# Cross attention in a decoder layer: passing two chunks through each stage together, and an output projection ordered by input chunk

## The chip, the cores and the metric

One core of one Trainium2 chip. The metric is the device time of one execution of the whole program, in microseconds (us). The engines are PE (matrix multiply; PEld is its weight load), DVE, ACT and POOL (elementwise and reductions) and SP (DMA issue). They run their own instruction streams and meet only at semaphores.

## The reference

A post-norm decoder layer on x (8 batches of 256 rows of 128): a state-space block, then cross attention, then six window-attention layers with feed-forward parts. Only the cross attention is touched. For each batch it computes, with 16 heads of 64:

```
lat = layernorm(latents, ln_l_w, ln_l_b)
ctx = layernorm(context, ln_c_w, ln_c_b)
q = (lat @ Wq).reshape(b, n, H, D).transpose(0, 2, 1, 3)
kv = ctx @ Wkv
...
attn = jnp.einsum('bhnd,bhsd->bhns', q, k) * scale
attn = jnp.clip(attn, -11.0, 11.0)
attn = jax.nn.softmax(attn, axis=-1)
out = jnp.einsum('bhns,bhsd->bhnd', attn, v)
out = out.transpose(0, 2, 1, 3).reshape(b, n, INNER)
return out @ Wo + bo
...
x = _layernorm(x + _L0_xattn_ref(x, ctx_1024, ...), axis=-1)
```

## The kernel before

The three blocks run one after the other; at the end of each, all engines meet. The cross-attention block is a software pipeline, written out by hand for each engine, over 64 chunks g: 8 batches b of 8 chunks c, a chunk being two heads (128 of the 1024 inner columns). All of it is in 32-bit floats. The names used below for the stages of a chunk on PE are these:

- P(g), `project`, L966 and L967: q and k of the chunk, two matmuls of 128x256 on the full 128x128 array, into one of two shared PSUM banks psM. ACT copies the bank to qk (`copy_qk`, L852).
- S(g), `scores`, L982: four matmuls of 256 columns, each on 64 rows of the array, so that two heads run side by side. ACT takes the exponential into E (`exponentials`, L845, two instructions), DVE clips it (`clip`, L899), and POOL adds the two key tiles into Es (L794).
- T(g), `times_v`: four matmuls with weights of 64 columns (L997), two side by side, then two with a matrix of ones (L1001) that sum the rows. DVE takes the reciprocal and multiplies (`normalise`, L903 and L904), which fills OT and counts O_free.
- V, `project_v`, L973: one 512-column matmul on the full array, once in each chunk with c of 4 to 7 for the next batch; ACT copies it (L836).
- OP, `out_projection`, L1012: 2x8 matmuls of 128 columns per batch, from OT and wo. DVE adds the result to res (`residual`, L909), takes moments (L47, L51), and `finish` (L918) writes the batch back. TR, `transpose_rows`, L958, prepares the next batch from `hats` (L893), which needs `statistics` (L47, L51) and ACT's `deviation` (L818, L819).

In iteration g PE does P(g+1), S(g), T(g-1). At the start of a batch, OP for the first tile of rows of the batch before comes at the end of the iteration with c = 1, and for the second tile at c = 2. E, Es, qk and psO have two buffers each, psS has four banks. The table `fills` lists everything that is put into the two psM banks, in PE's order; entry k goes into bank k mod 2, and PE may start it only when the entry before it in that bank has been read out (`bank`, `place`).

Of the kernel before, what the change touches and what calls it, by code (L numbers as in the profile page):

```python
# [680 lines left out]
def cross_attention_block(nc, xall, ident, eps_col, inputs, window):  # L681
# [9 lines left out]
    R = 2 * TPB  # L691
    LOADS = 16 * 7
    CHUNKS = B * NC
    LO, HI = float(np.exp(-11.0)), float(np.exp(11.0))

    with ExitStack() as ctx:
        def sb(name, shape, dt=F32):
            return ctx.enter_context(nc.sbuf_tensor(name, shape, dt))
# [48 lines left out]

        block = ctx.enter_context(nc.Block())

        fills = [(0, "cat"), (0, "qk0")]  # L750
        for g in range(CHUNKS + 1):
            b, c = divmod(g, NC)
            if g + 1 < CHUNKS:
                fills.append(((g + 1) // NC, f"qk{(g + 1) % NC}"))
            if g == 0:
                fills += [(0, f"v{n}") for n in range(4)]
            if c == 1 and b >= 1:
                fills.append((b - 1, "wo"))
            if c == 3 and b + 1 < B:
                fills.append((b + 1, "cat"))  # L760
            if c >= 4 and b + 1 < B:
                fills.append((b + 1, f"v{c - 4}"))
        fills.append((B - 1, "wo"))
        place = {f: (k % 2, k // 2) for k, f in enumerate(fills)}

        def wait_fill(eng, b, name):
# [16 lines left out]
        @block.gpsimd  # L783
        def _(pool):
            pool.memset(ones[:, :], 1.0).then_inc(Es_ready, 1)
            pool.memset(window.xsA[0:1, 0, 64:D], 0.0)
            pool.wait_ge(loaded, LOADS)

            def sum_of_tiles(g):
                pool.wait_ge(E_ready, 2 * g + 2)  # L790
                if g >= 2:

                    pool.wait_ge(O_full, g - 1)
                pool.tensor_tensor(Es[:, g % 2, :, :], E[:, g % 2, :, 0, :], E[:, g % 2, :, 1, :], ALU.add).then_inc(Es_ready, 1)  # L794
# [12 lines left out]
            pool.wait_ge(window.loaded, 32)  # L807
            pool.tensor_scalar(window.base_tab[:, :, 0, :, :], window.base_tab[:, :, 0, :, :], 8.0, None, ALU.mult)

        @block.scalar  # L810
        def _(act):
# [27 lines left out]
            def exponentials(g):  # L839
                for j in range(2):  # L840
                    act.wait_ge(S_full, 2 * g + j + 1)
                    if j == 0 and g >= 2:

                        act.wait_ge(O_full, g - 1)
                    act.activation(E[:, g % 2, j, :, :], psS[(2 * g + j) % 4][:, :, :], ACT.Exp, scale=DH ** -0.5).then_inc(E_exp, 1)  # L845
# [8 lines left out]
            deviation(0)  # L854
            scale_transposed(0)
            copy_qk(0)
            for g in range(CHUNKS + 1):
                b, c = divmod(g, NC)
                if g + 1 < CHUNKS:
                    copy_qk(g + 1)  # L860
                if g < CHUNKS:
                    exponentials(g)
                if g == 0:
                    for n in range(4):
                        evacuate_v(0, n)
                if c == 1 and b + 1 < B:
                    deviation(b + 1)
                if c == 3 and b >= 1:
                    deviation2(b - 1)
                if c == 3 and b + 1 < B:  # L870
                    scale_transposed(b + 1)
                if c >= 4 and b + 1 < B:
                    evacuate_v(b + 1, c - 4)
            deviation2(B - 1)

        @block.vector
        def _(dve):
# [18 lines left out]
            def clip(g):  # L896
                for j in range(2):
                    dve.wait_ge(E_exp, 2 * g + j + 1)
                    dve.tensor_scalar(E[:, g % 2, j, :, :], E[:, g % 2, j, :, :], LO, HI, ALU.max, ALU.min).then_inc(E_ready, 1)  # L899

            def normalise(g):
                dve.wait_ge(O_full, g + 1)
# [1 line left out]
                dve.tensor_tensor(OT[:, g // NC % 2, g % NC, :], psO[g % 2][:, 0, :], rden[:, g % 2, :], ALU.mult).then_inc(O_free, 1)  # L904

            def residual(b):
                ps, free = wait_fill(dve, b, "wo")
                dve.wait_ge(res_ready, b + 1)
                dve.tensor_tensor(res[:, :, :], res[:, :, :], ps[:, 0:TPB * D].rearrange("p (t d) -> p t d", d=D), ALU.add).then_inc(free, 1)  # L909

            def moments2(b):
                wait_evacuated(dve, b, "wo")
# [7 lines left out]

            statistics(0)
            hats(0)
            for g in range(CHUNKS + 1):
                b, c = divmod(g, NC)
                if c == 2 and b >= 1:
# [7 lines left out]
                if c == 2 and b + 1 < B:  # L933
                    hats(b + 1)
                if c == 2 and b >= 1:
                    moments2(b - 1)
                if c == 4 and b >= 1:
                    finish(b - 1)
            residual(B - 1)
            moments2(B - 1)  # L940
# [3 lines left out]
        def _(pe):  # L944
# [41 lines left out]
            def times_v(g):  # L986
                b, c = divmod(g, NC)
                pe.wait_ge(E_ready, 2 * g + 2)
                if c == 0:
                    for n in range(4):  # L990
                        wait_evacuated(pe, b, f"v{n}")
                if g >= 2:

                    pe.wait_ge(O_free, g - 1)
                for kt in range(TPB):
                    for j in range(2):
                        pe.matmul(psO[g % 2][j * DH:(j + 1) * DH, 0, :], V1[:, b % 2, kt, 2 * c + j, :], E[:, g % 2, j, kt, :],  # L997
                                  start=(kt == 0), stop=(kt == TPB - 1), skip_group_check=True)
# [19 lines left out]
            for g in range(CHUNKS + 1):  # L1018
# [10 lines left out]
                if g >= 1:  # L1029
# [3 lines left out]
                if c == 3 and b + 1 < B:  # L1033
# [979 lines left out]
```

## Time and profile before

| what | value |
|---|---|
| median of 3 timed runs | 2367.09 us (2366.22 to 2367.36) |
| the profiled execution, its own time | 2364.26 us |
| span of its trace | 2362.5 us |
| PE busy share of the span | 93% |
| cross attention, about | 321 to 623 us of the span |

The profile page gives, for the whole span, busy time and instruction count of each engine. Everything else is read from the stretch of the cross attention: the timeline (instructions in order of time, with start and length), the table of stretches, and the list of waits. In the timeline, runs of like matmuls are merged into one row; a row ends with a modelled tail, so distances are taken from start to start. A float matmul is shown as two records, so that `x8` of L982 is a whole S.

### The profile page before, as it was taken

Reading aid. Unit: us, or ns where it says so; the run is one execution under the profiler, and the core shown is the slowest. Engines: PE = TensorE matmul, PEld = TensorE weight load, DVE = VectorE, ACT = ScalarE, POOL = GpSimd, SP = SyncE. Lnnn points to the kernel's source line nnn. Section 1 sums busy time; section 2 is a strip of 40 time slices with the busy share of each in tenths; the row PEclk is TensorE's granted clock in tenths of the full one; section 3 lists DMA queues with packets and bytes.
Section 4 is the critical chain, followed back from the end, with each engine's and each line's share of the span. In section 5 each row is a group of like instructions: output and inputs, shape, how many; then the busy total and the mean of one; then the engine's idle time right before and its main releaser. Section 6 shows DMA issues by size and latency. Waiting matters only on the chain. (4 is left out here: it accounts for less than half of the span.)

```text
span 2362.5 us, 70312 instructions
## 1 busy us (share of the span) xinstructions
PE 2204.0 (93%) x26385; PEld 1467.1 (62%) x26385; DVE 1860.9 (79%) x2680; ACT 1707.2 (72%) x3299; POOL 1648.2 (70%) x1553
## 2 busy tenths in 40 slices
PE   5889779999799999999999999999999999999996
PEld 3555446666456666666666666666666666666664
DVE  4899957777678878888888888888888887888884
ACT  5889734544377787787787787787778778778774
POOL 4777833333478778778788787787787787787872
PEclk8999989999999999999999999999999999999997
DMA  2311210000022222222222222222222222322221
GB/s 74 113 58 66 72 52 2 1 1 1 20 63 67 55 78 67 59 74 67 65 69 67 69 64 67 73 60 67 77 55 68 79 54 68 79 53 72 75 53 52
DMA packets 103196, 140.36 MB, mean 59 GB/s; under 512 B 63072, under 2 KB 64096, under 8 KB 102752
## 3 DMA queue, kind: packets, MB, share of 16 engines
q1 hardware_dynamic: 103136, 139.57, 21.8%
q8 instruction: 36, 0.59, 0.1%
q14 instruction: 24, 0.20, 0.0%
HBM read 56.39 MB, written 1.31 MB: 24 GB/s over the span
## 5 line engine op out<-in xcount | busy, mean ns | idle before, releaser
L1802 PE MATMUL f_psA<-f_W,f_xT 128*128 (+1 forms) x1152 | 600.7, 631 | 21.1 <-DVE f_m L1607 13.4
L1607 DVE TENSOR_TENSOR f_m<-f_psA,f_tab 128x1024 f32<-128x1024 f32 x384 | 461.1, 1222 | 119.5 <-ACT f_sq L1468 106.3
L1357 POOL TENSOR_TENSOR f_Pr<-f_Pr,f_rden 128x384 f32<-128x384 f32 x384 | 311.0, 831 | 226.2 <-DVE f_rden L1586 226.2
L1385 POOL TENSOR_TENSOR f_qkr<-f_qkr,f_rn 128x1024 f32<-128x1024 f32 x192 | 361.2, 1902 | 0.2 <-POOL f_rn L1393 0.2
L1802 PEld LDWEIGHTS f_psA<-f_W,f_xT 128*128 128x128 f32 x1152 | 188.3, 189 | 162.9 <-issue 112.5
L1468 ACT ACTIVATE f_sq<-f_psA 128x512 f32<-128x512 f32 x384 | 228.0, 594 | 78.6 <-PE f_psA L1802 75.7
L1773 PEld LDWEIGHTS f_psO<-f_PT,f_V 96*64 96x64 f32 x6144 | 203.7, 138 | 96.5 <-issue 88.4
L1375 POOL TENSOR_TENSOR f_qkr<-f_m 128x512 f32<-128x512 f32 x192 | 244.1, 1271 | 8.2 <-DVE f_m L1607 8.2
L1376 POOL TENSOR_TENSOR f_qkr<-f_m 128x512 f32<-128x512 f32 x192 | 244.5, 1273 | 0.0
L1773 PE MATMUL f_psO<-f_PT,f_V 96*64 96x64 f32 x6144 | 232.1, 228 | 1.8 <-ACT f_PT L1443 1.8
L794 POOL TENSOR_TENSOR x_Es<-x_E 128x512 f32<-128x512 f32 x64 | 81.0, 1266 | 205.8 <-DVE x_E L899 205.8
L1622 DVE TENSOR_REDUCE f_ssq<-f_sq 128x32 f32<-128x2048 f32 x96 | 218.5, 2276 | 0.0
L1460 ACT ACTIVATE f_Pr<-f_Pr 128x768 f32<-128x768 f32 x192 | 162.2, 845 | 55.4 <-DVE f_Pr L1580 53.8
L1869 PE MATMUL f_psO<-f_W,f_oT 128*128 (+1 forms) x1536 | 196.9, 281 | 0.8 <-ACT f_oT L1456 0.8
L284 POOL TENSOR_TENSOR m_Hs<-m_Hs,m_Cb 128x1024 f32<-128x1024 f32 x64 | 151.3, 2370 | 64.4 <-DVE m_Hs L472 64.4
L1452 ACT ACTIVATE f_Vt<-f_psA 128x512 f32<-128x512 f32 x192 | 114.5, 597 | 112.0 <-PE f_psA L1802 107.1
L1580 DVE TENSOR_TENSOR f_Pr<-f_psS,f_mx 128x768 f32<-128x768 f32 x192 | 183.8, 957 | 10.7
L1573 DVE TENSOR_REDUCE f_mx<-f_psS 128x8 f32<-128x768 f32 x192 | 178.3, 929 | 14.3 <-PE f_psS L1741 8.6
L1869 PEld LDWEIGHTS f_psO<-f_W,f_oT 128*128 128x128 f32 x1536 | 178.7, 191 | 7.3 <-issue 0.9
L1584 DVE TENSOR_REDUCE f_den<-f_Pr 128x8 f32<-128x768 f32 x192 | 179.9, 937 | 3.9 <-ACT f_Pr L1460 3.9
L1417 POOL TENSOR_SCALAR f_hatC<-f_xsC,f_momC,f_rstdC 128x128 f32<-128x128 f32 x96 | 77.1, 803 | 136.9 <-ACT f_rstdC L1544 136.9
L1806 PE MATMUL f_psD<-f_xnT,f_W 128*128 128x256 f32 (+1 forms) x576 | 163.6, 395 | 1.4 <-issue 0.8
(167 smaller groups left out, 4894.6 us busy)
## 6 DMA issues: line engine op xcount, KB each, us to landing
f_V<-f_Vt SPq DMA_DIRECT2D x96, 384.0 KB, 4.2
f_V<-f_Vt SPq DMA_DIRECT2D x96, 256.0 KB, 3.6
f_W<-in_f_W SPq DMA_DIRECT2D x48, 344.0 KB, 3.4
m_Cb<-m_BC_rows SPq DMA_DIRECT2D x64, 256.0 KB, 3.1
f_W<-in_f_W SPq DMA_DIRECT2D x48, 296.5 KB, 4.0
f_V<-f_Vt SPq DMA_DIRECT2D x48, 128.0 KB, 5.3
f_xsA<-xall SPq DMA_DIRECT2D x97, 32.0 KB
f_xsA<-xall SPq DMA_DIRECT2D x97, 31.8 KB
```

Source lines behind the costliest of these rows:

```text
L1357: pool.tensor_tensor(pv, pv, rv.unsqueeze(3).broadcast_to([P, 2, 2, KEYS]), ALU.mult).then_inc(Pr_ready[g][j], 1)
L1375: pool.tensor_tensor(qv[:, :, 0, :], mv[:, 0, :, 0, :], mv[:, 1, :, 1, :], ALU.add)
L1376: pool.tensor_tensor(qv[:, :, 1, :], mv[:, 0, :, 1, :], mv[:, 1, :, 0, :], ALU.add).then_inc(rot_done[j], 1)
L1385: pool.tensor_tensor(qv, qv, rv.unsqueeze(3).broadcast_to([P, 2, GH, DH]), ALU.mult).then_inc(qkr_ready[g], 1)
L1468: act.activation(sq[:, n * 512:(n + 1) * 512], psA[n % 2][:, :], ACT.Square).then_inc(squared[n], 1)
L1580: dve.tensor_tensor(Pr[:, g, :, :].rearrange("p (a c) k -> p a c k", a=2), S4, mb, ALU.subtract).then_inc(S_free[g], 1)
L1584: dve.tensor_reduce(den[:, g, :], Pr[:, g, :, :], axis=AX.X, op=ALU.add).then_inc(den_done[g], 1)
L1607: dve.tensor_tensor(m12[:, j, :, half].rearrange("p m (h d) -> p m h d", d=DH), psA[n % 2][:, :].rearrange("p (h d) -> p h d", d=DH).unsqu ...
L1622: dve.tensor_reduce(ssq[:, :], sq[:, :].rearrange("p (h d) -> p h d", d=DH), axis=AX.X, op=ALU.add).then_inc(ssq_ready, 1)
L1773: ins = pe.matmul(psO[(h % 2) * DH:(h % 2) * DH + DH, h // 2, half * HQ:(half + 1) * HQ], V96[:, tile, half, hh_ * DH:(hh_ + 1) * DH], PT[ ...
L1802: pe.matmul(psA[n % 2][:, :], xT[:, t, :], weights(i, W_QKV + n * 512, 512), start=True, stop=True).then_inc(A_full[n_fill], 1)
L1869: ins = pe.matmul(psO[:, 0, :], oT[:, t, c, :], weights(i - 1, W_O + c * D, D), start=(c == 0), stop=(c == CH - 1))
```

## The change

Chunks pass the stages in pairs. In iteration g (now in steps of two) PE does S(g), S(g+1), T(g-2), T(g-1), P(g+2), P(g+3), then TR or two V where a batch has them. E has four buffers (ES = 4) where it had two. OP stands as one piece at the start of the iteration with c = 2; it goes over the eight input chunks in order, each time for both tiles of rows, and each tile has a psM bank of its own (`wo0`, `wo1`). It waits for both banks first and then for each chunk's O_free. The orders of `fills`, ACT and DVE follow; DVE does `clip(g)`, `normalise(g-2)`, `clip(g+1)`, `normalise(g-1)`, has `hats` before `residual` at c = 2, and `residual` is two instructions.

```diff
-        E = sb("x_E", [P, 2, 2, TPB, L])
+        E = sb("x_E", [P, ES, 2, TPB, L])
...
-        fills = [(0, "cat"), (0, "qk0")]
-        for g in range(CHUNKS + 1):
+        fills = [(0, "cat"), (0, "qk0"), (0, "qk1")]
+        for g in range(0, CHUNKS + 1, 2):
             b, c = divmod(g, NC)
-            if g + 1 < CHUNKS:
-                fills.append(((g + 1) // NC, f"qk{(g + 1) % NC}"))
+            if c == 2 and b >= 1:
+                fills += [(b - 1, f"wo{t}") for t in range(TPB)]
             if g == 0:
                 fills += [(0, f"v{n}") for n in range(4)]
-            if c == 1 and b >= 1:
-                fills.append((b - 1, "wo"))
-            if c == 3 and b + 1 < B:
+            if g + 2 < CHUNKS:
+                fills += [((g + 2) // NC, f"qk{(g + 2) % NC}"), ((g + 3) // NC, f"qk{(g + 3) % NC}")]
+            if c == 2 and b + 1 < B:
                 fills.append((b + 1, "cat"))
...
@@ ACT
-            for g in range(CHUNKS + 1):
+            for g in range(0, CHUNKS + 1, 2):
                 b, c = divmod(g, NC)
-                if g + 1 < CHUNKS:
-                    copy_qk(g + 1)
                 if g < CHUNKS:
                     exponentials(g)
+                    exponentials(g + 1)
                 if g == 0:
                     for n in range(4):
                         evacuate_v(0, n)
-                if c == 1 and b + 1 < B:
+                if g + 2 < CHUNKS:
+                    copy_qk(g + 2)
+                    copy_qk(g + 3)
+                if c == 0 and b + 1 < B:
                     deviation(b + 1)
...
@@ PE
-            def out_projection(b, t):
-                if t == 0:
-                    pe.wait_ge(O_free, (b + 1) * NC)
-                    ps, full = bank(b, "wo")
-                else:
-                    j = place[b, "wo"][0]
-                    ps, full = psM[j], misc_full[j]
+            def out_projection(b):
+                places = [bank(b, f"wo{t}") for t in range(TPB)]
                 for c in range(NC):
-                    ins = pe.matmul(ps[:, t * D:(t + 1) * D], OT[:, b % 2, c, t * P:(t + 1) * P], wo[:, c, :], start=(c == 0), stop=(c == NC - 1))
-                if t == TPB - 1:
-                    ins.then_inc(full, 1)
+                    pe.wait_ge(O_free, b * NC + c + 1)
+                    for t in range(TPB):
+                        ps, full = places[t]
+                        ins = pe.matmul(ps[:, 0:D], OT[:, b % 2, c, t * P:(t + 1) * P], wo[:, c, :], start=(c == 0), stop=(c == NC - 1))
+                        if c == NC - 1:
+                            ins.then_inc(full, 1)
...
-            for g in range(CHUNKS + 1):
+            for g in range(0, CHUNKS + 1, 2):
                 b, c = divmod(g, NC)
-                if g + 1 < CHUNKS:
-                    project(g + 1)
                 if c == 2 and b >= 1:
-                    out_projection(b - 1, 1)
+                    out_projection(b - 1)
                 if g < CHUNKS:
                     scores(g)
+                    scores(g + 1)
                 if g == 0:
                     for n in range(4):
                         project_v(0, n)
-                if g >= 1:
+                if g >= 2:
+                    times_v(g - 2)
                     times_v(g - 1)
-                if c == 1 and b >= 1:
-                    out_projection(b - 1, 0)
-                if c == 3 and b + 1 < B:
+                if g + 2 < CHUNKS:
+                    project(g + 2)
+                    project(g + 3)
+                if c == 2 and b + 1 < B:
                     transpose_rows(b + 1)
                 if c >= 4 and b + 1 < B:
                     project_v(b + 1, c - 4)
-            out_projection(B - 1, 0)
-            out_projection(B - 1, 1)
+                    project_v(b + 1, c - 3)
+            out_projection(B - 1)
```

The first place is PE's stream in the second half of a batch. Before, two iterations (c = 6 and 7):

```order
L973 MATMUL x_psM<-x_wv,x_ctxT 128x512
L966 MATMUL x_psM<-x_latT,x_wq 128x256
L967 MATMUL x_psM<-x_ctxT,x_wk 128x256
L982 MATMUL x_psS<-x_qk 128x256 x4
L997 MATMUL x_psO<-x_E,x_V 64x256 x4
L1001 MATMUL x_psO<-x_Es,x_ones 64x256 x2
L973 MATMUL x_psM<-x_wv,x_ctxT 128x512
L966 MATMUL x_psM<-x_latT,x_wq 128x256
L967 MATMUL x_psM<-x_ctxT,x_wk 128x256
L982 MATMUL x_psS<-x_qk 128x256 x4
L997 MATMUL x_psO<-x_E,x_V 64x256 x4
L1001 MATMUL x_psO<-x_Es,x_ones 64x256 x2
```

Now, one iteration for the same work (P is L977 and L978, S L993, T L1008 and L1012, V L984):

```order
L993 MATMUL x_psS<-x_qk 128x256 x8
L1008 MATMUL x_psO<-x_E,x_V 64x256 x4
L1012 MATMUL x_psO<-x_Es,x_ones 64x256 x2
L1008 MATMUL x_psO<-x_E,x_V 64x256 x4
L1012 MATMUL x_psO<-x_Es,x_ones 64x256 x2
L977 MATMUL x_psM<-x_latT,x_wq 128x256
L978 MATMUL x_psM<-x_ctxT,x_wk 128x256
L977 MATMUL x_psM<-x_latT,x_wq 128x256
L978 MATMUL x_psM<-x_ctxT,x_wk 128x256
L984 MATMUL x_psM<-x_wv,x_ctxT 128x512 x2
```

The two S stand together, as do the two T and the two P, so PE passes from one kind of work to the next three times where it did so six times.

The second place is PE at the turn from c = 0 to c = 2 of the next batch. Before, from the last T of a batch (OP is L1012):

```order
L997 MATMUL x_psO<-x_E,x_V 64x256 x4
L1001 MATMUL x_psO<-x_Es,x_ones 64x256 x2
L1012 MATMUL x_psM<-x_wo,x_OT 128x128 x8
L966 MATMUL x_psM<-x_latT,x_wq 128x256
L967 MATMUL x_psM<-x_ctxT,x_wk 128x256
L1012 MATMUL x_psM<-x_wo,x_OT 128x128 x8
L982 MATMUL x_psS<-x_qk 128x256 x4
```

Now (OP is L1021):

```order
L1008 MATMUL x_psO<-x_E,x_V 64x256 x4
L1012 MATMUL x_psO<-x_Es,x_ones 64x256 x2
L977 MATMUL x_psM<-x_latT,x_wq 128x256
L978 MATMUL x_psM<-x_ctxT,x_wk 128x256
L977 MATMUL x_psM<-x_latT,x_wq 128x256
L978 MATMUL x_psM<-x_ctxT,x_wk 128x256
L1021 MATMUL x_psM<-x_wo,x_OT 128x128 x16
L993 MATMUL x_psS<-x_qk 128x256 x8
```

OP is now one piece directly behind two P, and all three write the two psM banks.

The third place is DVE over the same turn, from the batch's last `normalise`. Before:

```order
L904 TENSOR_TENSOR x_OT<-x_psO,x_rden 128x256
L47 BN_STATS x_stats<-xall 128x6 x2
L47 BN_STATS x_stats<-x_ctx 128x6 x2
L51 BN_AGGR x_mom<-x_stats 128x2 x4
L899 TENSOR_SCALAR x_E<-x_E 128x512 x2
L903 RECIPROCAL x_rden<-x_psO 128x256
L904 TENSOR_TENSOR x_OT<-x_psO,x_rden 128x256
L909 TENSOR_TENSOR x_res<-x_res,x_psM 128x256
L899 TENSOR_SCALAR x_E<-x_E 128x512 x2
```

Now (`clip` is L904, the multiply of `normalise` L909):

```order
L909 TENSOR_TENSOR x_OT<-x_psO,x_rden 128x256
L47 BN_STATS x_stats<-xall 128x6 x2
L47 BN_STATS x_stats<-x_ctx 128x6 x2
L51 BN_AGGR x_mom<-x_stats 128x2 x4
L898 TENSOR_SCALAR x_hat<-xall,x_mom,x_rstd 128x128 x2
L898 TENSOR_SCALAR x_hat<-x_ctx,x_mom,x_rstd 128x128 x2
L915 TENSOR_TENSOR x_res<-x_res,x_psM 128x128 x2
L904 TENSOR_SCALAR x_E<-x_E 128x512 x2
```

`statistics`, `hats` and `residual` now follow each other with no chunk's work between them.

## Rows read from the trace of the kernel before

**Rows 1.** The page, whole span: busy us (share), instructions of each engine.

```profile
PE 2204.0 (93%) x26385; PEld 1467.1 (62%) x26385; DVE 1860.9 (79%) x2680; ACT 1707.2 (72%) x3299; POOL 1648.2 (70%) x1553
```

**Rows 2.** Table of stretches, two of the cross attention's six; columns as in its first line.

```profile
core 0: us, PE busy (x) PEld busy (x) DVE busy (x) ACT busy (x) POOL busy (x), PEclk, DMA share, GB/s
350.00:400.00 50.00, 50.00 (x321) 30.66 (x318) 36.41 (x66) 24.66 (x47) 14.65 (x13) 1.00 0.01 2
550.00:600.00 50.00, 50.00 (x340) 32.92 (x340) 36.37 (x68) 23.08 (x45) 14.61 (x12) 1.00 0.00 1
```

**Rows 3.** Timeline of PE, one chunk with V: start us, length us, engine, line.

```profile
350.43 1.13 PE L973 MATMUL x_psM<-x_wv,x_ctxT 128*128 128x512 f32 x2
351.39 0.59 PE L966 MATMUL x_psM<-x_latT,x_wq 128*128 128x256 f32 x2
351.82 0.59 PE L967 MATMUL x_psM<-x_ctxT,x_wk 128*128 128x256 f32 x2
352.35 1.14 PE L982 MATMUL x_psS<-x_qk 64*128 64x256 f32 x8
353.41 1.08 PE L997 MATMUL x_psO<-x_E,x_V 128*64 128x256 f32 x8
354.32 0.60 PE L1001 MATMUL x_psO<-x_Es,x_ones 128*64 128x256 f32 x4
354.86 1.13 PE L973 MATMUL x_psM<-x_wv,x_ctxT 128*128 128x512 f32 x2
```

**Rows 4.** Waits, 330 to 614 us: who waited for whom, total us, times, longest.

```profile
PEld x_psO L997 <- issue: 20.9, 63, 0.3
```

**Rows 5.** Timeline of PE where OP's second half stands.

```profile
374.04 0.59 PE L967 MATMUL x_psM<-x_ctxT,x_wk 128*128 128x256 f32 x2
374.47 1.95 PE L1012 MATMUL x_psM<-x_wo,x_OT 128*128 128x128 f32 x16
376.35 1.14 PE L982 MATMUL x_psS<-x_qk 64*128 64x256 f32 x8
```

**Rows 6.** Timeline of the other engines beside the chunk of rows 3.

```profile
352.45 0.60 ACT L852 ACTIVATE x_qk<-x_psM 128x512 f32<-128x512 f32 x1 [0.27 <-PE x_psM L967]
353.51 1.09 ACT L845 ACTIVATE x_E<-x_psS 128x512 f32<-128x512 f32 x2 [0.46 <-PE x_psS L982]
354.14 0.92 DVE L899 TENSOR_SCALAR x_E<-x_E 128x512 f32<-128x512 f32 x2 [1.38 <-ACT x_E L845]
354.97 1.76 DVE L903 RECIPROCAL x_rden<-x_psO 128x256 f32<-128x256 f32 x1
355.14 1.26 POOL L794 TENSOR_TENSOR x_Es<-x_E 128x512 f32<-128x512 f32 x1 [3.16 <-DVE x_E L899]
356.77 0.42 DVE L904 TENSOR_TENSOR x_OT<-x_psO,x_rden 128x256 f32<-128x256 f32 x1
```

**Rows 7.** Timeline of DVE, the work at a batch's start.

```profile
370.39 0.47 DVE L47 BATCH_NORM_STATS2 x_stats<-xall 128x6 f32<-128x128 f32 x2
...
371.70 0.73 DVE L899 TENSOR_SCALAR x_E<-x_E 128x512 f32<-128x512 f32 x2
...
381.11 0.59 DVE L893 TENSOR_SCALAR x_hat<-xall,x_mom,x_rstd 128x128 f32<-128x128 f32 x2
...
382.92 0.73 DVE L899 TENSOR_SCALAR x_E<-x_E 128x512 f32<-128x512 f32 x2
```

**Rows 8.** Timeline of the end of the cross attention: S(62), last O_free, OP, moments.

```profile
606.40 1.13 PE L982 MATMUL x_psS<-x_qk 64*128 64x256 f32 x8
...
615.81 0.42 DVE L904 TENSOR_TENSOR x_OT<-x_psO,x_rden 128x256 f32<-128x256 f32 x1
616.29 3.65 PEld L1012 LDWEIGHTS x_psM<-x_wo,x_OT 128*128 128x128 f32 x32 [2.77 <-DVE x_OT L904]
...
620.62 0.49 DVE L47 BATCH_NORM_STATS2 x_stats<-x_res 128x6 f32<-128x128 f32 x2
```

**Rows 9.** Table of stretches, behind the cross attention; columns as in rows 2.

```profile
626.00:630.00 4.00, 2.45 (x6) 0.82 (x6) 3.28 (x4) 1.50 (x3) 2.01 (x2) 1.00 0.04 9
634.00:638.00 4.00, 3.12 (x4) 0.83 (x4) 0.56 (x1) 3.47 (x6) 3.82 (x4) 0.67 0.44 90
638.00:642.00 4.00, 3.28 (x4) 1.12 (x4) 2.26 (x3) 1.04 (x2) 2.54 (x3) 0.50 0.28 90
```

More of the change, by code:

```diff
@@ L693, in cross_attention_block @@
     CHUNKS = B * NC
+    ES = 4
     LO, HI = float(np.exp(-11.0)), float(np.exp(11.0))
@@ L748, in cross_attention_block @@
         block = ctx.enter_context(nc.Block())
-        fills = [(0, "cat"), (0, "qk0")]
-        for g in range(CHUNKS + 1):
+        fills = [(0, "cat"), (0, "qk0"), (0, "qk1")]
+        for g in range(0, CHUNKS + 1, 2):
             b, c = divmod(g, NC)
-            if g + 1 < CHUNKS:
-                fills.append(((g + 1) // NC, f"qk{(g + 1) % NC}"))
+            if c == 2 and b >= 1:
+                fills += [(b - 1, f"wo{t}") for t in range(TPB)]
             if g == 0:
                 fills += [(0, f"v{n}") for n in range(4)]
-            if c == 1 and b >= 1:
-                fills.append((b - 1, "wo"))
-            if c == 3 and b + 1 < B:
+            if g + 2 < CHUNKS:
+                fills += [((g + 2) // NC, f"qk{(g + 2) % NC}"), ((g + 3) // NC, f"qk{(g + 3) % NC}")]
+            if c == 2 and b + 1 < B:
                 fills.append((b + 1, "cat"))
             if c >= 4 and b + 1 < B:
-                fills.append((b + 1, f"v{c - 4}"))
-        fills.append((B - 1, "wo"))
+                fills += [(b + 1, f"v{c - 4}"), (b + 1, f"v{c - 3}")]
+        fills += [(B - 1, f"wo{t}") for t in range(TPB)]
         place = {f: (k % 2, k // 2) for k, f in enumerate(fills)}
@@ L793, in sum_of_tiles @@
                     pool.wait_ge(O_full, g - 1)
-                pool.tensor_tensor(Es[:, g % 2, :, :], E[:, g % 2, :, 0, :], E[:, g % 2, :, 1, :], ALU.add).then_inc(Es_ready, 1)
+                pool.tensor_tensor(Es[:, g % 2, :, :], E[:, g % ES, :, 0, :], E[:, g % ES, :, 1, :], ALU.add).then_inc(Es_ready, 1)
             def add_bias(b):
@@ L841, in exponentials @@
                     act.wait_ge(S_full, 2 * g + j + 1)
-                    if j == 0 and g >= 2:
-                        act.wait_ge(O_full, g - 1)
-                    act.activation(E[:, g % 2, j, :, :], psS[(2 * g + j) % 4][:, :, :], ACT.Exp, scale=DH ** -0.5).then_inc(E_exp, 1)
+                    if j == 0 and g >= ES:
+                        act.wait_ge(O_full, g - ES + 1)
+                    act.activation(E[:, g % ES, j, :, :], psS[(2 * g + j) % 4][:, :, :], ACT.Exp, scale=DH ** -0.5).then_inc(E_exp, 1)
             def copy_qk(g):
@@ L865, in _ @@
                         evacuate_v(0, n)
-                if c == 1 and b + 1 < B:
+                if g + 2 < CHUNKS:
+                    copy_qk(g + 2)
+                    copy_qk(g + 3)
+                if c == 0 and b + 1 < B:
                     deviation(b + 1)
-                if c == 3 and b >= 1:
+                if c == 2 and b + 1 < B:
+                    scale_transposed(b + 1)
+                if c == 4 and b >= 1:
                     deviation2(b - 1)
-                if c == 3 and b + 1 < B:
-                    scale_transposed(b + 1)
                 if c >= 4 and b + 1 < B:
                     evacuate_v(b + 1, c - 4)
+                    evacuate_v(b + 1, c - 3)
             deviation2(B - 1)
@@ L898, in clip @@
                     dve.wait_ge(E_exp, 2 * g + j + 1)
-                    dve.tensor_scalar(E[:, g % 2, j, :, :], E[:, g % 2, j, :, :], LO, HI, ALU.max, ALU.min).then_inc(E_ready, 1)
+                    dve.tensor_scalar(E[:, g % ES, j, :, :], E[:, g % ES, j, :, :], LO, HI, ALU.max, ALU.min).then_inc(E_ready, 1)
             def normalise(g):
@@ L906, in residual @@
             def residual(b):
-                ps, free = wait_fill(dve, b, "wo")
                 dve.wait_ge(res_ready, b + 1)
-                dve.tensor_tensor(res[:, :, :], res[:, :, :], ps[:, 0:TPB * D].rearrange("p (t d) -> p t d", d=D), ALU.add).then_inc(free, 1)
+                for t in range(TPB):
+                    ps, free = wait_fill(dve, b, f"wo{t}")
+                    dve.tensor_tensor(res[:, t, :], res[:, t, :], ps[:, 0:D], ALU.add).then_inc(free, 1)
             def moments2(b):
-                wait_evacuated(dve, b, "wo")
+                for t in range(TPB):
+                    wait_evacuated(dve, b, f"wo{t}")
                 layer_norm_stats(dve, passed, mom2_ready, chain, [res[:, j, :] for j in range(TPB)], stats2, mom2)
@@ L922, in _ @@
             hats(0)
-            for g in range(CHUNKS + 1):
+            for g in range(0, CHUNKS + 1, 2):
                 b, c = divmod(g, NC)
+                if c == 2 and b + 1 < B:
+                    hats(b + 1)
                 if c == 2 and b >= 1:
@@ L928, in _ @@
                     clip(g)
-                if g >= 1:
+                if g >= 2:
+                    normalise(g - 2)
+                if g < CHUNKS:
+                    clip(g + 1)
+                if g >= 2:
                     normalise(g - 1)
@@ L932, in _ @@
                     statistics(b + 1)
-                if c == 2 and b + 1 < B:
-                    hats(b + 1)
                 if c == 2 and b >= 1:
                     moments2(b - 1)
-                if c == 4 and b >= 1:
+                if c == 6 and b >= 1:
                     finish(b - 1)
@@ L996, in times_v @@
                     for j in range(2):
-                        pe.matmul(psO[g % 2][j * DH:(j + 1) * DH, 0, :], V1[:, b % 2, kt, 2 * c + j, :], E[:, g % 2, j, kt, :],
+                        pe.matmul(psO[g % 2][j * DH:(j + 1) * DH, 0, :], V1[:, b % 2, kt, 2 * c + j, :], E[:, g % ES, j, kt, :],
                                   start=(kt == 0), stop=(kt == TPB - 1), skip_group_check=True)
@@ L1002, in times_v @@
                 ins.then_inc(O_full, 1)
-            def out_projection(b, t):
-                if t == 0:
-                    pe.wait_ge(O_free, (b + 1) * NC)
-                    ps, full = bank(b, "wo")
-                else:
-                    j = place[b, "wo"][0]
-                    ps, full = psM[j], misc_full[j]
-                for c in range(NC):
-                    ins = pe.matmul(ps[:, t * D:(t + 1) * D], OT[:, b % 2, c, t * P:(t + 1) * P], wo[:, c, :], start=(c == 0), stop=(c == NC - 1))
-                if t == TPB - 1:
-                    ins.then_inc(full, 1)
+            def out_projection(b):
+                places = [bank(b, f"wo{t}") for t in range(TPB)]
+                for c in range(NC):
+                    pe.wait_ge(O_free, b * NC + c + 1)
+                    for t in range(TPB):
+                        ps, full = places[t]
+                        ins = pe.matmul(ps[:, 0:D], OT[:, b % 2, c, t * P:(t + 1) * P], wo[:, c, :], start=(c == 0), stop=(c == NC - 1))
+                        if c == NC - 1:
+                            ins.then_inc(full, 1)
             transpose_rows(0)
             project(0)
-            for g in range(CHUNKS + 1):
+            project(1)
+            for g in range(0, CHUNKS + 1, 2):
                 b, c = divmod(g, NC)
-                if g + 1 < CHUNKS:
-                    project(g + 1)
                 if c == 2 and b >= 1:
-                    out_projection(b - 1, 1)
+                    out_projection(b - 1)
                 if g < CHUNKS:
                     scores(g)
+                    scores(g + 1)
                 if g == 0:
@@ L1028, in _ @@
                         project_v(0, n)
-                if g >= 1:
+                if g >= 2:
+                    times_v(g - 2)
                     times_v(g - 1)
-                if c == 1 and b >= 1:
-                    out_projection(b - 1, 0)
-                if c == 3 and b + 1 < B:
+                if g + 2 < CHUNKS:
+                    project(g + 2)
+                    project(g + 3)
+                if c == 2 and b + 1 < B:
                     transpose_rows(b + 1)
```

1 line of the change is left out of this document (added).

## The prediction

> **What bounds the kernel now.** The page comes first: PE is busy 93% of the span, the next engine 79% [rows 1]. The change touches only the cross attention, so I read the table of stretches there: PE is busy 50.00 of 50.00 us at the full clock, DVE some 36.4, ACT 23 to 25, POOL 15 [rows 2]. PE sets the pace, so the timeline of PE tells what a chunk costs. From V to V are 354.86 - 350.43 = 4.43 us [rows 3]. The unit is one matmul of 256 columns in steady flow: L966 to L967 is 0.43 us. S is four matmuls but two run side by side, so two units; so is T's first part; the ones are one unit, P two, V two: nine units, 3.87 us. So 0.56 us of each chunk is something else, though PE never reads idle. Start to start against units, it stands at the borders: V takes 0.96 (0.10 over), L966 0.43 (nothing), L967 before S 0.53 (0.10), S 1.06 (0.20), L997 0.91 (0.05), the ones 0.54 (0.11). It is paid where the shape of the weights changes between 128x128, 64x128 and 128x64, on leaving one and on entering the next, and nowhere between two stages of one shape. V to P costs nothing, although P has a semaphore wait of its own (`bank`); L967 to OP costs 0.43, nothing either [rows 5]. The list of waits puts the weight load's part of it to "issue", 63 times for L997 [rows 4], so no other engine is waited for.
>
> The Trainium skill says the same in TensorEngine Tiling (Array Packing), Key Properties: changing the tiling mode, not just the tile, drains the engine. By that rule the pairs would save 17.4 us in all; if each stage paid, whatever its shape, nothing.
>
> **The change part by part.**
>
> *Pairs on PE.* The matmuls stay the same in number and size. Three changes of shape per chunk become three per pair: 0.56 us less per pair. That S(g) to S(g+1) and T to the next T cost nothing is not in the trace; the nearest rows are V to P and P to OP, at 0 to 0.01 [rows 3, 5]; the other bound is that a second stage of the same kind pays all of 0.56. I take nothing. With 31 pairs ahead of the tail: -17.4 us. A pair without V lasts 14 x 0.43 + 0.56 = 6.6 us, one with V 8.3.
>
> *A wait ahead of OP.* OP now asks for both psM banks first, and the two P right before it filled them. Let the P pair start at s. The second P's L967 starts at s + 0.10 + 3 x 0.43 = s + 1.39 and ends at s + 1.83. ACT's copy starts 0.63 after L967 (351.82 to 352.45) and takes 0.60 [rows 3, 6]: s + 2.02 to s + 2.62. A PE that waits for another engine's result starts some 0.06 behind it (616.23 to 616.29) [rows 8]: s + 2.68. PE stands 0.85 us. This happens for 7 batches, 7 x 0.85 = +5.95 us. Behind the waiting OP are S(g) and so all of the batch's next work, and nothing covers it. Elsewhere the same arithmetic gives no wait: V's first and TR need the bank of the first P, read out at s + 1.77 + 0.06, when PE arrives at s + 1.83; V's second needs the other bank at 2.68 and comes at 1.83 + 0.86. Margins are nil there, but a miss costs hundredths.
>
> *OP's wait for O_free.* Put zero at S(g). T(g-2) starts at 4 x 0.43 + 0.20 = 1.92, its ones at 2.83; the reciprocal follows 0.65 later (354.32 to 354.97) at 3.48, the multiply 1.80 later (354.97 to 356.77) at 5.28 [rows 6]. The multiply to the next instruction takes at most 0.42, and a clip 0.83 (354.14 to 354.97): DVE does clip(g+1) 5.7 to 6.5, normalise(g-1) 6.5 to 8.75. The batch's last O_free is so 2.2 us into the next iteration, where OP (starting at 0.75) has 14 matmuls of 0.22 (8 in 1.88 - 0.10 [rows 5]), 3.1 us, to do before it needs that. Hidden. OP itself has the same 16 matmuls: 0.
>
> *DVE.* A chunk costs it 0.83 + 1.80 + 0.42 = 3.05, a pair 6.1 of PE's 6.6. Statistics add 1.31 (370.39 to 371.70), hats and moments 1.81 (381.11 to 382.92) [rows 7], residual and finish about 0.5 each (an estimate from the 0.42 of a like instruction). The statistics so end at 10.1, that is 3.5 into the c = 2 iteration; with ACT's two short instructions (0.6, an estimate) hats end about 5.2, residual 5.7. But S(g) there waits behind OP until 4.4; its exponential starts 1.16 later (352.35 to 353.51) and the clip 0.63 after that (353.51 to 354.14) [rows 3, 6]: 6.2. DVE is free by then. From there clip to 7.0, the reciprocal of the first T at 4.4 + 3.48 = 7.9, then 2.2 + 0.83 + 2.2 + 0.8 for the moments: 13.9. That iteration has 6.6 + 3.6 + 0.85 + TR's 0.4 (an estimate) = 11.4 on PE, so DVE is 2.5 into the next, where clip ends at 3.3, ahead of the reciprocal's 3.48; normalise(g-1) ended at 1.7, and the T that needs it starts at 3.3. I cost DVE at nothing; the cover is 0.2 us at the one place and 1.6 at the other.
>
> *ACT and POOL.* Four exponentials end near 3.3 (1.16 + 4 x 0.55), the copies are due at 5.8: idle between. Es(g+1) starts 1.0 after its clip and ends at 8.0 [rows 6], the ones that read it start at 10.7. Four E buffers only let ACT go ahead. Nothing.
>
> *Start and tail.* At g = 0 the V copies stand behind two more exponentials (1.09 us) while PE has one more S (1.06): even. In the tail S(62) stands at 606.40 and the moments at 620.62: 14.2 us [rows 8]. Now from S(62): T(60) at 1.9, its O_free 5.8, T(62) there, as psO has two buffers; T(63) waits for O_free(61) at 8.7 and its ones start at 9.6. DVE then normalises 62 (8.6 to 10.8) and 63 (10.8 to 13.0). Fourteen of OP's 16 matmuls run from 10.1 to 13.4 beside that, the last two end at 13.9, moments near 14.5. At S(62) PE has T(60), 1.3 us, still ahead of it, which was done before. So the tail gives 1.3 - 0.3 = 1.0: -1.0 us.
>
> **The sum.** -17.4 + 5.95 - 1.0 = -12.4 us against the profiled execution's 2364.3 (span 2362.5): 2351.9. The median of the runs is 2.8 above that execution, so I expect a median of 2354.7. All engines meet behind the block, so what it saves the program saves.
>
> **The rivals.**
>
> *The border cost stays in part (0.16).* A second S or T may pay, since the weights of a 64-row tile can only be loaded when that tile is free. For it: S shows 0.20 over and the trace has no two S in a row. Against: inside S and T the tiles alternate at no cost. Half of it left gives -8.7 + 5.95 - 1.0 = -3.7: 2363.4.
>
> *No wait at OP (0.10).* If the copy were sooner or the border at P longer, the 5.95 would be gone: 2348.7. Against it stands the 0.63 of rows 3 and 6, the same in each chunk.
>
> *DVE or ACT becomes late at a batch's start (0.09).* Statistics, hats and residual now follow each other. If 0.5 to 1 us of this reaches PE in 7 batches: 3.5 to 7 us, 2358 to 2362. The working above has 0.2 us to spare where it is tightest.
>
> *Slower (0.05): the border is the price of every stage, whatever its shape.* Then the pairs save nothing, and the new wait ahead of OP remains: +5.95 - 1.0 = +4.95, 2372. It decides once less than 4.95 / 31 = 0.16 of the 0.56 is saved per pair. V to P without any cost speaks against it.
>
> *The clock.* Behind the block the granted clock falls from 1.00 to 0.50 around 638 us, after stretches with PE busy 2.45 of 4.00 [rows 9]. If an altered tail moves or removes that stretch, some 6 us at 1.2 GHz instead of 2.4 are worth up to 3 us either way. It widens the range only.
>
> **How the numbers follow.** The forecast case has 0.60 and spans 2349 to 2358. What a measurement can tell from no change is about 0.2%, 4.7 us. Faster by more: the forecast, the missing wait, most of the late DVE, a part of the first rival: 0.84. Within: most of the first rival and some of the third: 0.11. Slower: 0.05. The range of 2346 to 2363 takes in the missing wait with some clock, and half of the border left.
>
> **What would show it.** In the timeline of PE a pair without V should last 6.6 us and one with V 8.3; S(g) to S(g+1) 0.86 more and not 1.06; OP behind P with a wait of 0.85 for ACT's copy, 7 times; a batch 6.6 + 11.4 + 2 x 8.3 = 34.6 us, where it was 4 x 4.43 + 4 x 3.57 + 3.6 + 0.4 = 36.0. The stretches should show DVE busy near 38 of 50. In the tail OP starts before the last normalise ends. The prediction is wrong if S or T in a row show a gap, if T waits for O_free in c = 0 or 2, or if OP's wait is absent.

## The result, and the profile after

The changed kernel's median is 2362.57 us (2360.04 to 2363.53, 19 runs). The kernel before, timed beside it, has 2366.63 us (2365.32 to 2370.92, 19 runs). The ratio is 0.998 with a 95% interval of 0.9973 to 0.9987: faster by 4.1 us where 12.4 were forecast. The profiled execution took 2361.96 us with a span of 2360.2, so 2.3 less than before in its own time as in its span.

The page's first part, and the row of DVE's costliest group:

```profile
PE 2193.8 (93%) x26385; PEld 1474.2 (62%) x26385; DVE 1861.7 (79%) x2688; ACT 1705.1 (72%) x3299; POOL 1650.7 (70%) x1553
...
L1618 DVE TENSOR_TENSOR f_m<-f_psA,f_tab 128x1024 f32<-128x1024 f32 x384 | 461.5, 1222 | 125.2 <-ACT f_sq L1479 108.5
```

PE reads 93% as before [rows 1], and nothing on the page says what changed. The second row belongs to the window layers, whose text the change doesn't touch. Its idle time, the third field, was 119.5 us before (L1607 there). That the untouched part waits 5.7 us longer is the first hint.

**The cross attention.** The timeline of PE, from a pair (c = 0) over OP to the next (c = 2), in place of [rows 3, 5]:

```profile
362.62 2.00 PE L993 MATMUL x_psS<-x_qk 64*128 64x256 f32 x16
364.55 1.08 PE L1008 MATMUL x_psO<-x_E,x_V 128*64 128x256 f32 x8
365.47 0.60 PE L1012 MATMUL x_psO<-x_Es,x_ones 128*64 128x256 f32 x4
365.90 1.03 PE L1008 MATMUL x_psO<-x_E,x_V 128*64 128x256 f32 x8
366.76 0.60 PE L1012 MATMUL x_psO<-x_Es,x_ones 128*64 128x256 f32 x4
367.29 0.70 PE L977 MATMUL x_psM<-x_latT,x_wq 128*128 128x256 f32 x2
367.83 0.59 PE L978 MATMUL x_psM<-x_ctxT,x_wk 128*128 128x256 f32 x2
368.26 0.59 PE L977 MATMUL x_psM<-x_latT,x_wq 128*128 128x256 f32 x2
368.69 0.59 PE L978 MATMUL x_psM<-x_ctxT,x_wk 128*128 128x256 f32 x2
370.02 3.81 PE L1021 MATMUL x_psM<-x_wo,x_OT 128*128 128x128 f32 x32 [0.73 <-issue]
373.76 2.00 PE L993 MATMUL x_psS<-x_qk 64*128 64x256 f32 x16
...
380.90 2.00 PE L993 MATMUL x_psS<-x_qk 64*128 64x256 f32 x16
...
389.36 2.00 PE L993 MATMUL x_psS<-x_qk 64*128 64x256 f32 x16
...
397.76 2.00 PE L993 MATMUL x_psS<-x_qk 64*128 64x256 f32 x16
...
405.16 3.81 PE L1021 MATMUL x_psM<-x_wo,x_OT 128*128 128x128 f32 x32 [0.73 <-issue]
```

Two S in a row take 364.55 - 362.62 = 1.93 us: four units of 0.43 and one border of 0.20. From the first T's ones to the second T is 0.43, no border. OP starts 1.33 after the last L978, of which 0.43 is that matmul: PE stands 0.90 us (the row's 0.73 counts from the modelled end of the matmul before). A batch, OP to OP, is 35.14 us; it was 371.71 to 407.68, 35.97.

The row calls the wait "issue", since the semaphore is taken by the weight load. The list of waits from 330 to 614 us (total us, times, longest) names who was waited for:

```profile
PEld x_psM L984 <- ACT x_qk L853: 9.1, 21, 0.6
PEld x_psM L1021 <- ACT x_qk L853: 7.7, 7, 1.1
...
PE x_psM L1021 <- issue: 5.1, 7, 0.7
```

OP waits for ACT's copy in each of 7 batches. L984 is V: its load too now waits for ACT's copy of q and k, 21 times, which it did nowhere in the same list of the kernel before. PEld runs ahead of PE, so only part of such a wait is PE's: OP's load waits 7.7 us in all, its matmul 5.1.

**The tail and what follows.** The timeline of PE from the last two S pairs (the second is S(62) and S(63)), the last moments on DVE, and the timeline of PE again, into the first window layer:

```profile
591.19 2.00 PE L993 MATMUL x_psS<-x_qk 64*128 64x256 f32 x16
...
597.78 2.00 PE L993 MATMUL x_psS<-x_qk 64*128 64x256 f32 x16
...
607.88 3.93 PE L1021 MATMUL x_psM<-x_wo,x_OT 128*128 128x128 f32 x32
```

```profile
610.62 0.42 DVE L909 TENSOR_TENSOR x_OT<-x_psO,x_rden 128x256 f32<-128x256 f32 x1
...
612.28 0.49 DVE L47 BATCH_NORM_STATS2 x_stats<-x_res 128x6 f32<-128x128 f32 x2
```

```profile
614.69 0.30 PE L1708 MATMUL f_psD<-ident,f_xsA 128*128 128x128 f32 x1 [2.88 <-PEq L697]
615.36 3.41 PE L1813 MATMUL f_psA<-f_W,f_xT 128*128 128x512 f32 x4 [0.37 <-ACT f_xT L1445]
```

The same two rows of the kernel before:

```profile
623.03 0.30 PE L1697 MATMUL f_psD<-ident,f_xsA 128*128 128x128 f32 x1 [2.90 <-PEq L696]
623.69 1.98 PE L1802 MATMUL f_psA<-f_W,f_xT 128*128 128x512 f32 x4 [0.37 <-ACT f_xT L1434]
```

The moments stand at 612.28, where they stood at 620.62 [rows 8]: the cross attention gives 8.34 us, and the window layers start 623.03 - 614.69 = 8.34 sooner. But their first four matmuls take 3.41 us instead of 1.98. The table of stretches (length, then busy time of PE, PEld, DVE, ACT, POOL, the granted clock, DMA) for these four microseconds after, and then before:

```profile
614.00:618.00 4.00, 2.94 (x4) 1.31 (x5) 2.23 (x10) 0.81 (x2) 0.72 (x1) 0.61 0.39 101
```

```profile
622.00:626.00 4.00, 2.28 (x5) 0.82 (x5) 2.90 (x11) 1.23 (x4) 0.72 (x1) 1.00 0.39 98
```

The granted clock is 0.61, where it was 1.00: part of the stretch at 1.2 GHz, not 2.4. In both kernels PE had just been idle for some 2.9 us. At DVE's last `f_ssq` ahead of the window loop's first branch (705.26 against 712.36) the lead is 7.10, so 1.2 us are lost for good here. One of the runs below shows the same slow stretch behind the old cross attention: the kernel before with 256 more instructions on DVE early in the program, which enters its window layers 4.57 us later, at 627.59:

```profile
628.41 3.78 PE L1806 MATMUL f_psA<-f_W,f_xT 128*128 128x512 f32 x4 [0.37 <-ACT f_xT L1438]
```

So the pairs are not needed for it; what decides it is open.

**The window loop.** DVE's `f_ssq` (one per half step of the loop, 54 of them between these two) after, then before:

```profile
1253.37 2.28 DVE L1633 TENSOR_REDUCE f_ssq<-f_sq 128x32 f32<-128x2048 f32 x1
...
2207.39 2.27 DVE L1633 TENSOR_REDUCE f_ssq<-f_sq 128x32 f32<-128x2048 f32 x1
```

```profile
1258.66 2.28 DVE L1622 TENSOR_REDUCE f_ssq<-f_sq 128x32 f32<-128x2048 f32 x1
...
2209.74 2.28 DVE L1622 TENSOR_REDUCE f_ssq<-f_sq 128x32 f32<-128x2048 f32 x1
```

954.02 us against 951.08 for the same work. The lead of the changed kernel is 5.29 at the first of them and 2.35 at the second, and it shrinks evenly, by 0.1 us in each of the 27 iterations between them. It is lost at one place on DVE, once per iteration. After, then before:

```profile
1282.17 0.20 DVE L1597 RECIPROCAL f_rden<-f_den 128x8 f32<-128x8 f32 x1
1282.76 2.36 DVE L1618 TENSOR_TENSOR f_m<-f_psA,f_tab 128x1024 f32<-128x1024 f32 x2 [0.39 <-ACT f_sq L1479]
```

```profile
1287.46 0.20 DVE L1586 RECIPROCAL f_rden<-f_den 128x8 f32<-128x8 f32 x1
1287.95 2.35 DVE L1607 TENSOR_TENSOR f_m<-f_psA,f_tab 128x1024 f32<-128x1024 f32 x2 [0.29 <-issue]
```

From the reciprocal to the multiply are 0.59 us instead of 0.49. Between the two stands the end of the loop's body: DVE compares a counter and branches back (`eng.Fori(2, ITERS)`). The trace's own record of the branch says it to the nanosecond: from the branch to DVE's next record are 183 ns before and 288 ns after, in the median of its 46 branches. The other engines' branches keep their time (SP 172 and 173, ACT 228, POOL 256 ns, PE 265 and 266). The last of the 46 does not jump back, so the loss is 45 x 0.105 = 4.7 us.

So the span: -8.34 + 1.2 (clock) + 4.7 (DVE's branch) = -2.4, where it measures -2.3.

What could lengthen a branch whose code is the same? DVE's program ahead of it: the trace records 1210 DVE instructions ahead of the loop's first branch before and 1226 after, since `residual` is two instructions and DVE's waits and counts are arranged otherwise. My theory was that the place of the loop in DVE's program sets the price. The rivals: that the altered timing of the engines does it, or that more instructions simply cost more.

### The profile page after: what moved, and what is told of

It reads as the page before. It is cut to its first block and busy times, and to the rows that moved or that the text cites. A ratio compares the mean times of both kernels' runs of the same rounds, so it can differ in the third digit from the quotient of the medians.

```text
span 2360.2 us, 70326 instructions
## 1 busy us (share of the span) xinstructions
PE 2193.8 (93%) x26385; PEld 1474.2 (62%) x26385; DVE 1861.7 (79%) x2688; ACT 1705.1 (72%) x3299; POOL 1650.7 (70%) x1553
## 5 line engine op out<-in xcount | busy, mean ns | idle before, releaser
L1752 PE MATMUL f_psS<-f_qkT 64*64 64x96 f32 x6144 | 164.1, 243 | 0.0
```

## The experiments

Each kernel of a group ran beside the kernel before. "Increments" are bare counts of a semaphore on DVE, `alone(dve, passed)`, that nothing new waits on and that leave the computation as it is.

**1. The place of the loop alone.** To the kernel before, 16 increments in a long wait of DVE early in the program, ahead of the cross attention. The same edit in the changed kernel.

```diff
+            for _ in range(16):
+                alone(dve, passed)
```

> The kernel before, with 16 bare semaphore increments (nothing waits on them) put on DVE in its wait for the first loads, so that DVE's window loop stands where it stands in the changed kernel: 16 instructions later. Theory (the place of DVE's code sets what the jump back of the loop costs): the step behind DVE's loop branch goes from 183 to about 287 ns in each of 46 iterations, the distance of two landmarks 36 slots apart grows by 1.9 us, and the run is 4.8 us longer than before, about 2371.4. Rival (the longer loop is a matter of when the window layers are entered, that is of the phase and the clock): no change, 2366.6, and 183 ns. The increments themselves are hidden in a wait of 5.1 us.

> The changed kernel with 16 such increments, 32 places beyond the kernel before. By the theory of place the step behind DVE's loop branch may change again: if it goes by some block of 32 or fewer instructions, back to 183 ns and 4.8 us less than the changed kernel (2357.8); if the block is larger, it stays near 287 ns and 2362.6. Rival (time of entry): unchanged, 2362.6.

The kernel before with 16 increments: 2369.7 us (2368.77 to 2372.2, 11 runs) against 2367.01 (27 runs), ratio 1.0011 [1.0002, 1.002]; span 2367.0. The rows at the same place of the loop as above:

```profile
1289.25 0.20 DVE L1588 RECIPROCAL f_rden<-f_den 128x8 f32<-128x8 f32 x1
1289.84 2.35 DVE L1609 TENSOR_TENSOR f_m<-f_psA,f_tab 128x1024 f32<-128x1024 f32 x2 [0.39 <-issue]
```

The step is 0.59 us, the branch 288 ns, and the 54 half steps take 953.88 us, all as in the changed kernel, though the cross attention is the old one and its window layers start at 622.93, where they did within 0.1. This falsifies the rival of the altered timing. The median rises by 2.7 us, not by the 4.8 that were expected. With 16 more, the changed kernel stays at 288 ns and 2362.35 us (ratio 0.998 [0.9971, 0.9989], span 2360.0): 32 more instructions cost no more than 16.

**2. The same from the other side.** In the changed kernel, the 16 bare increments that follow the statistics of the cross attention are left out; nothing waits on them.

```diff
-    alone(dve, passed)
+    if own:
+        alone(dve, passed)
...
-                layer_norm_stats(dve, passed, mom_ready, chain, rows_of(b), stats, mom)
+                layer_norm_stats(dve, passed, mom_ready, chain, rows_of(b), stats, mom, own=False)
```

> The changed kernel without the 16 bare semaphore increments that DVE does in the cross attention ahead of each averaging of moments (nothing waits on them), so that DVE's window loop stands where it stands in the kernel before. Theory of place: the step behind the loop's branch is back at 183 ns, and the run is 46 x 0.104 = 4.8 us shorter than the changed kernel, 2357.8. Rival (something else in the changed kernel's DVE code makes the branch slow): 287 ns and 2362.6.

2359.19 us (2356.38 to 2360.45, 9 runs) against 2366.09 (13 runs), ratio 0.9971 [0.9961, 0.9981]; span 2354.6. The changed kernel's own ratio, from another group, is 0.998 [0.9973, 0.9987]: the two intervals overlap, so it is the trace that decides here. The branch is at 183 ns again, and the 54 half steps at 951.13 us:

```profile
1250.76 2.28 DVE L1634 TENSOR_REDUCE f_ssq<-f_sq 128x32 f32<-128x2048 f32 x1
...
1279.57 0.20 DVE L1598 RECIPROCAL f_rden<-f_den 128x8 f32<-128x8 f32 x1
1280.05 2.36 DVE L1619 TENSOR_TENSOR f_m<-f_psA,f_tab 128x1024 f32<-128x1024 f32 x2 [0.28 <-ACT f_sq L1480]
...
2201.89 2.28 DVE L1634 TENSOR_REDUCE f_ssq<-f_sq 128x32 f32<-128x2048 f32 x1
```

The step is 0.48 us and the lead no longer shrinks: 7.90 us at the first `f_ssq`, 7.85 at the second. Here no part of the gain is lost in the loop. (The window layers start at 614.17, 8.86 us sooner than in the kernel before and 0.5 sooner than in the changed one, and the slow first stretch is there too: their first four matmuls take 3.78.)

**3. Other places.** The kernel before with 4, 8, 64, 128 and 256 increments, and without the 16. One timed run each.

> The kernel before with 4 increments on DVE in its first wait; one look at the step behind DVE's loop branch. 0 gives 183 ns and 8 gives 288. If there is one edge between them, this lies on either side of it; it narrows the edge to 4 places.

> The kernel before with 8 increments on DVE ahead of the first loads, one look to see how fine the dependence on place is. If the step behind the branch changes at some place between 0 and 16, it is 183 or 287 ns, by the side of it; if it follows the place in steps, something between.

> The kernel before with 64 increments on DVE, 48 in the wait for the first loads and 16 in the next wait. If the place matters modulo 64 or a divisor of it, 183 ns; if by a larger block, 287 ns or so as with 16 and 32.

> The kernel before with 128 increments (52 in the first wait, 76 in the second, where some of them are not hidden, so that the whole is 1 to 2 us longer for that). Looked at for the branch only: 183 ns if the place matters modulo 128, 288 ns if by a larger block or by a single edge.

> As with 128, now 256 increments, of which many are not hidden (the run is some 14 us longer for that). 183 ns if the place matters modulo 256, 288 ns if not.

> The kernel before without the cross attention's 16 bare increments on DVE, so 16 places earlier. If there is one edge between 0 and 8, this is on the fast side with 0: 183 ns, and the time is that of the kernel before within 1 us. If 0 is a lucky place, 288 ns and 4.8 us more.

DVE's step after the branch (median of the 46, from the trace's records), with the one run's time; the kernels before beside them have 2366.09 and, for the four that are marked, 2365.45 us:

```
increments   -16*     0     +4*     +8    +16    +64   +128*   +256*
step, ns     191    183    160    288    288    288    183     183
one run   2364.96     -  2365.81 2369.7 2369.7 2368.41 2365.22 2369.98
span       2363.2 2362.5 2364.0 2367.9 2367.0 2366.6  2363.4  2368.2
```

(+16 is the median and the profile of experiment 1.) In the changed kernel itself, at +16, the step is 288 ns, at +32 288 and without the 16, at 0, 183. The step takes four values, the dearest starts between 4 and 8 more instructions, and the value of 0 comes back at 128 and at 256. The 160 at +4 and the 191 at -16 were not among the expected values, and a single edge between 0 and 8 is out. The run with 256 has no drift in the loop; it is 4.5 us longer, not the 14 that were expected, because not all of its increments lie in idle time: its window layers start 4.57 us later and lose another 1.1 in the slow stretch shown above. So the place matters, not the count. What in the hardware sets the price, a boundary that the branch or its target crosses for one, isn't shown: eight places are too few to tell.

**4. The wait ahead of OP.** The changed kernel, with OP in another order: chunks 0 to 3 of the first tile after its own bank alone, then 0 to 3 of the second after the other bank, then 4 to 7 of both. The same 16 matmuls.

```diff
-                places = [bank(b, f"wo{t}") for t in range(TPB)]
-                for c in range(NC):
-                    pe.wait_ge(O_free, b * NC + c + 1)
-                    for t in range(TPB):
+                places = {}
+                for cs, ts in [(range(0, 4), (0,)), (range(0, 4), (1,)), (range(4, NC), (0, 1))]:
+                    for t in ts:
+                        if t not in places:
+                            places[t] = bank(b, f"wo{t}")
+                    for c in cs:
+                        pe.wait_ge(O_free, b * NC + c + 1)
+                        for t in ts:
```

> The changed kernel with the same OP matmuls in another order: the first tile's chunks 0 to 3, after a wait for its bank alone, then the second tile's chunks 0 to 3 after a wait for the other bank, then chunks 4 to 7 for both. The second bank is read out 0.85 us after PE's arrival, and four matmuls last 0.89 us. Theory (the two bank waits ahead of OP are what PE stands for, 0.90 us at each of 7 batches): the wait vanishes, a batch lasts 34.2 us in place of 35.14, 6.3 us less in all, 2356.3. Rival (OP in truth waits for the last normalised chunks, O_free): the 0.90 us only move, 0 to 1 us less.

2354.33 us (2353.39 to 2356.79, 5 runs), ratio 0.9947 [0.9933, 0.9961], span 2354.0. The timeline of PE around OP, and OP of the batch before:

```profile
403.85 3.83 PE L1025 MATMUL x_psM<-x_wo,x_OT 128*128 128x128 f32 x32
...
437.67 0.59 PE L978 MATMUL x_psM<-x_ctxT,x_wk 128*128 128x256 f32 x2
438.10 3.83 PE L1025 MATMUL x_psM<-x_wo,x_OT 128*128 128x128 f32 x32
441.86 1.35 PE L993 MATMUL x_psS<-x_qk 64*128 64x256 f32 x10
```

OP follows the last L978 by 0.43: the wait is gone. The batch is 34.25 us, 0.89 less, in each of seven, and the whole of the wait was on the path. (7 x 0.89 = 6.2 us; the span is 6.2 less and the median 8.2. The window layers start 5.7 sooner, at 608.99, since S(0) stands 0.41 later here, ahead of anything that the edit touches; single traces agree only to about that.)

**5. The pairs.** The changed kernel with PE in the order S(g), T(g-2), S(g+1), T(g-1), P, P: five changes of shape per pair of chunks instead of three.

> The changed kernel with PE's order S(g), T(g-2), S(g+1), T(g-1), P, P in place of S, S, T, T, P, P: the same matmuls, with two more changes of shape per pair, T to S and S to T. Theory (a change of shape costs, 0.21 and 0.15 us): 31 pairs x 0.36 = 11.2 us more than the changed kernel, 2373.8; a pair without V 6.94 us. Rival (it is each stage's own start that costs, whatever stands before it): no change, 2362.6.

2372.34 us (2370.36 to 2373.81, 11 runs), ratio 1.0022 [1.0013, 1.0031], span 2372.0. The timeline of PE:

```profile
413.26 1.14 PE L993 MATMUL x_psS<-x_qk 64*128 64x256 f32 x8
414.33 1.08 PE L1008 MATMUL x_psO<-x_E,x_V 128*64 128x256 f32 x8
415.24 0.60 PE L1012 MATMUL x_psO<-x_Es,x_ones 128*64 128x256 f32 x4
415.77 1.13 PE L993 MATMUL x_psS<-x_qk 64*128 64x256 f32 x8
416.84 1.08 PE L1008 MATMUL x_psO<-x_E,x_V 128*64 128x256 f32 x8
417.75 0.60 PE L1012 MATMUL x_psO<-x_Es,x_ones 128*64 128x256 f32 x4
418.28 0.70 PE L977 MATMUL x_psM<-x_latT,x_wq 128*128 128x256 f32 x2
```

S to T is 1.07, as in the kernel before, and the ones to the next S 0.53; the pair lasts 0.35 longer up to L977 (5.02 instead of 4.67 at 362.62). From S(0) to S(62), 30 pairs, PE takes 277.70 us instead of 267.07: 10.63 more, 0.35 a pair. The window layers start at 625.92, 11.23 us later, which looks like the expected 31 x 0.36 but is not: 1.46 of it lie ahead of S(0) (332.18 instead of 330.72), where the edit changes nothing, and the tail from S(62) to the moments is 0.86 shorter (13.64). Without the late start the block costs 9.8 more, and the medians are 9.8 apart. The Trainium skill, in TensorEngine Tiling (Array Packing), Key Properties, has a change of tiling mode drain the engine and names no price. The run agrees in that such a change costs something, about 0.18 us (60 changes for 10.63), and stages of one shape in a row cost nothing; a drain as such is in no row.

**6. Both together.** Experiments 2 and 4 in one kernel.

> The kernel with the split wait (2354.3) without the same 16 increments. Theory of place: 183 ns, 4.8 us less, 2349.5. Rival: 2354.3. This is the version that should beat both kernels by most.

2352.1 us (2349.8 to 2354.83, 5 runs), ratio 0.9942 [0.9928, 0.9955], span 2350.3, branch 183 ns: the fastest of all, 14 us under the kernel before, and 2.6 above the 2349.5 that were expected. Against experiment 4, which ran in another group with its branch at 287 ns, it is 2.2 us, with intervals of the ratios that overlap; in the spans it is 3.7. S(0) stands 0.64 later here than in experiment 4.

## Why the prediction was right and wrong

**Wrong: "All engines meet behind the block, so what it saves the program saves."** This step took 6.0 of the 10.1 us by which the profile's gain fell short, and it is the one that failed. The block did hand over what it had saved, 8.34 us. Then 1.2 us went in the first stretch behind it, at a granted clock of 0.61, and 4.7 us in a loop that the change doesn't touch. The latter is shown by runs: adding 16 bare increments to the kernel before gives it the loss in the loop, taking 16 away from the changed kernel removes it. The former is read from the traces; no run was made to test it. I had given the clock up to 3 us either way, at a later stretch, and hadn't thought of code ahead of a loop as a cost. The medians show less of it than the traces: 2.7 us in experiment 1 and 3.4 in experiment 2 (across groups), against 4.5 and 5.6 of span. The interval of experiment 1's ratio is 0.5 to 4.7 us, and a profiled execution is a single one; in experiment 2 it was the shortest of the nine, and 0.5 us of its lead come from the block. Sorted afterwards by the granted clock that each run lists, the runs at 0.982 and above give 3.5 us in both experiments (2365.71 to 2369.21, and 2363.14 down to 2359.64). So the firm figure is that of the loop itself, 105 ns at each of 45 jumps back, and what the median makes of it is known only to a few microseconds.

**Right: the price of a border.** A pair without V and without a wait lasts 597.78 - 591.19 = 6.59 us, where 6.6 were forecast and two chunks took 2 x 3.57 = 7.14: S,S and T,T in a row cost nothing. Experiment 5 puts two changes of shape into each pair again and loses 0.35 for them, 10.6 us over 30 pairs. The rivals of a border that stays in part and of a border at every stage are out. The time of the first of them, 2363.4, lies within 1 us of the median; that is chance, as its mechanism is absent.

**Right: the wait ahead of OP.** 0.90 us for a forecast of 0.85, 7 times, for ACT's copy. The arithmetic of the copy held to 0.05 (369.32 to 369.92, PE at 370.02). Experiment 4 confirms that nothing covers it.

**Mis-sized: "Margins are nil there, but a miss costs hundredths."** The cross attention gave 8.34 us instead of 12.4, and the missing 4.1 are 7 batches of 35.14 instead of 34.56. By iteration: c = 0 is 0.07 over its forecast, OP 0.08, c = 2 0.16, c = 4 0.17, c = 6 0.10. At c = 2 TR starts 0.51 after L978 instead of 0.43, at c = 4 the first V does, and a pair of V takes 1.89 and 1.90 instead of 1.83; the list of waits puts those of V to ACT's copies. A miss that was to cost hundredths so costs up to 0.1, at nearly every bank wait. OP is different: its 16 matmuls take 3.74 up to S where 3.66 were forecast from its two halves, and in experiment 4, where PE hadn't stood ahead of it, 3.76. So the stand ahead of it hardly lengthens it (though in experiment 4 the wait for the second bank lies inside OP); its order over both tiles and the waits for O_free inside it are left, and weren't tested. These terms are read from the trace, not from an experiment of their own.

**Right: DVE, ACT and POOL stay hidden.** From 330 to 600 us the list of waits has no PE and no PEld that waits for DVE or POOL. DVE is busy 37.9 of 50 us in the mean of the stretches from 350 to 600, where 38 were forecast.

**Right: the tail.** From S(62) to the moments 14.50 us were forecast, and 612.28 - 597.78 is 14.50; OP starts (607.88) before the last normalise ends (611.04).

## What to carry to other kernels

On PE, stages of one weight shape belong together: the border between shapes costs about 0.18 us here in the mean and that between like stages nothing, even across a semaphore; but see to it that the pair doesn't ask for a bank that the stage just ahead of it has filled, or order the work so that one bank's share hides the other's copy. A gain in one block is not the program's gain until the blocks behind it have been compared landmark by landmark. When untouched code gets slower, look at what stands ahead of its loops on each engine before looking at the data flow.

## What the hardware showed unexpectedly

- A loop's branch back on DVE costs 160, 183, 191 or 288 ns by the place of the loop in DVE's program, with the body unchanged; the value came back after 128 and 256 instructions. Over 45 jumps back, 4.7 us of the span.
- The granted clock behind a block was 0.61 in one kernel and 1.00 in the other after the same 2.9 us of idle PE, at the price of 1.2 us. The kernel before shows the slow stretch too when it arrives 4.57 us later (256 more instructions), not when it arrives 0.8 to 1.1 later (4, 8 and 128 more), and in part, 2.74 us for the four matmuls, in the run without the 16, which arrives within 0.02 of it; no run here tells what decides it.
